# A graph-and-experts kernel: the second expert layer scales its rows by weights stored beside them and adds them into the output by accumulating scatters, without a last combining stage

## The reference, cut to what matters

```python
x = x + L0_gnn(layernorm(x))     # attention over heads of gathered rows
x = x + L0_ffn(layernorm(x))     # 6 experts, hidden 256, 256, the best 2 by softmax
x = x + L1_gnn(layernorm(x))     # GAT over 100000 edges, segment sums
x = x + L1_ffn(layernorm(x))     # 8 experts, hidden 1024, the best 2:
#   top_w, top_i = top_k(xf @ Wg + bg, 2);  top_w = softmax(top_w)
#   out = sum over e of w_dense[:, e] * (gelu(xf @ W1[e] + b1[e]) @ W2[e] + b2[e])
```

## Time and profile before

| | |
|---|---|
| runs (3), median | 2874.93 us (2872.90 to 2878.44) |
| profiled execution | 2876.24 us |
| its span, first to last instruction | 2874.6 us |
| busy in the span: TensorE / VectorE / ACT / POOL | 2056.5 / 1554.9 / 936.1 / 1426.2 us |
| mean granted TensorE clock | 0.822 |
| DMA | 293.06 MB, mean 102 GB/s |

### The profile page before, as it was taken

One profiled execution on the slowest core, in us unless ns is written; L12 is line 12 of the kernel. 1 busy time (PEld: TensorE's weight loads), 2 busy tenths in 40 slices (PEclk: granted clock), 3 DMA queues, 4 the chain that ended last, 5 costly groups with the idle time before them and its releaser, 6 DMA issues. The chain is left out here.

```text
span 2874.6 us, 54757 instructions
## 1 busy us (share of the span) xinstructions
PE 2056.5 (72%) x13130; PEld 1850.7 (64%) x13131; DVE 1554.9 (54%) x4111; ACT 936.1 (33%) x2579; POOL 1426.2 (50%) x1463
## 2 busy tenths in 40 slices
PE   2623328998475888877888788786519999999990
PEld 2423217898354666666666666665519999999990
DVE  5366525665473655555555555556624545555445
ACT  1333315676241111111111111112315555555540
POOL 1257753434104777777777777773761223232230
PEclk9855558999686888888888888886559999999995
DMA  6312243333353444444444444443251222121117
GB/s 157 102 45 78 76 116 92 105 102 98 105 169 93 112 112 114 112 114 114 112 114 113 110 115 112 112 114 87 103 141 46 72 73 73 55 91 51 62 37 268
DMA packets 234820, 293.06 MB, mean 102 GB/s; under 512 B 101917, under 2 KB 185524, under 8 KB 234540
## 3 DMA queue, kind: packets, MB, share of 16 engines
q0 software_dynamic: 72016, 202.56, 24.3%
q1 hardware_dynamic: 149222, 76.37, 10.5%
q10 hardware_dynamic: 13544, 13.73, 1.4%
HBM read 214.72 MB, written 78.22 MB: 102 GB/s over the span
## 5 line engine op out<-in xcount | busy, mean ns | idle before, releaser
L1553 POOL DMA_INDIRECT at_G<-h_as,at_idx x850 | 807.1, 950 | 269.2 <-issue 266.7
L1704 PE MATMUL at_pAgg<-at_G,at_OH 128*128 128x260 f32 x1700 | 542.6, 485 | 159.8 <-DVE at_ACC L1602 95.5
L1704 PEld LDWEIGHTS at_pAgg<-at_G,at_OH 128*128 128x128 f32 x1700 | 404.8, 246 | 261.5 <-DVE at_G L1584 179.0
L1169 POOL DMA_INDIRECT expert_out<-e_ob,e_to x212 | 221.6, 1045 | 560.6 <-DVE e_ob L1380 392.4
L1304 ACT ACTIVATE e_full<-e_pH,g_bias_hidden 128x256 f32<-128x256 f32 x640 | 316.0, 494 | 357.4 <-PE e_pH L1202 344.6
L1662 ACT ACTIVATE at_OT<-at_pTr 128x384 f32<-128x384 f32 (+1 forms) x300 | 125.7, 470 | 657.2 <-PE at_pTr L1689 656.9
L1364 DVE TENSOR_TENSOR e_hT_low<-e_full,e_hT_high 128x256 fp32r<-128x256 f32 x536 | 263.2, 503 | 130.6 <-ACT e_hT_high L1305 130.5
L1584 DVE TENSOR_TENSOR at_G<-at_G,at_pIds 128x1536 f32<-128x1536 f32 x150 | 249.7, 1665 | 153.5 <-ACT at_pIds L1669 153.5
L1200 PE MATMUL e_pH<-e_xT_high,e_WA_high 128*128 128x256 f32 x1072 | 309.1, 288 | 3.9 <-DVE e_WA_low L1359 3.0
L1201 PE MATMUL e_pH<-e_xT_low,e_WA_high 128*128 128x256 f32 x1072 | 306.8, 286 | 0.0
L1202 PE MATMUL e_pH<-e_xT_high,e_WA_low 128*128 128x256 f32 x1072 | 305.0, 285 | 0.0
(11 more groups left out here) (301 smaller groups left out, 3635.7 us busy)
## 6 DMA issues: line engine op xcount, KB each, us to landing
e_xs<-slot_rows SPq DMA_DIRECT2D x109, 257.0 KB
at_G<-h_as,at_idx POOLq DMA_INDIRECT x850, 2.8
b_rows<-expert_out SPq DMA_DIRECT2D x14, 896.0 KB
f_rows<-expert_out ACTq DMA_DIRECT2D x14, 896.0 KB, 6.9
g_raw_first<-in_L_ffn_W_dram POOLq DMA_DIRECT2D x8, 1024.0 KB, 5.3
g_raw_last<-in_L_ffn_W_dram POOLq DMA_DIRECT2D x8, 1024.0 KB
xt_ar<-a_og SPq DMA_DIRECT2D x7, 910.0 KB, 4.5
h_as<-b_og SPq DMA_DIRECT2D x7, 910.0 KB, 4.2
```

Of the source, the lines that this page charges most:

```text
L1169: gp.indirect_dma_start(K.YS, bass.IndirectOffsetOnAxis(ap=to[b][:, s:s + 1], axis=0), ob[b][:, s, :], None).then_inc(sent[b], 16)
L1553: gp.indirect_dma_start(G[j][:, c, :], None, K.T1, bass.IndirectOffsetOnAxis(ap=idx[j][:, c:c + 1], axis=0)).then_inc(gathered[j], 16)
L1704: last = nc.tensor.matmul(pAgg[:, 0:DIM + 4], OH[j][:, c, :], G[j][:, c, :], start=(j == 0 and c == 0), stop=(j == NJ - 1 and c == CHUNKS[ ...
```

## The change

The second layer's slots get rows of 261 numbers: 256 features, the output row, the two experts chosen and their two weights. So both copies of a row are the same, and both scatters of a trip go out together, without `move`; the weights are worked out trip by trip in `place`, with an Exp on ACT (`shares`). While b1 runs, SP stores `K.X` to the output. In e1 VectorE picks the share of the tile's expert, ACT scales the product by it (`scale`), VectorE adds the bias times the share, and POOL's scatter adds the rows into the output in DRAM; rows beyond the last node are left out by the bounds check. As two scatters may meet in one row, each waits until the one before has landed. `finish` is gone.

In both layers POOL's trip splits the last weights before it loads others, and waits for the landing of the previous tile's scatters in each tile ahead of its own, not at the end of a pair. VectorE notes the output rows earlier in its trip. In b0 the rows have two buffers, and its loops on SP and VectorE are written out.

```diff
-WIDE = DIM + 1
+TO, WHICH, SHARE = DIM, DIM + 1, DIM + 3
+WIDE0, WIDE1 = DIM + 1, DIM + 5
...
+K.XS = {tag: dram(f"slot_rows_{tag}", [DUMP + 2 * P, wide]) for tag, wide in (("e0", WIDE0), ("e1", WIDE1))}
+K.out = out
+K.YS = dram("expert_out", [2 * NODEROWS + 2 * MT, DIM])
...
-finish(K, out)
...
+rows = sb("rows", [P, 2, 2, BODY, DIM])
...
 def load_results(sp, i):
-    freed(sp, rows_used, i * BODY)
+    b = i % 2
+    if i >= 2:
+        freed(sp, rows_used, i - 1)
     for k in range(2):
         a = i * (BODY * P) + k * NODEROWS
-        at = slice(a, a + BODY * P) if isinstance(i, int) else bass.ds(sp.snap(a), BODY * P)
-        sp.dma_start(rows[:, k, :, :], K.YS[at, :].rearrange("(t p) d -> p t d", p=P)).then_inc(rows_in, 16)
+        sp.dma_start(rows[:, b, k, :, :], K.YS[a:a + BODY * P, :].rearrange("(t p) d -> p t d", p=P)).then_inc(rows_in[b], 16)
...
+if gate:
+    with sp.Fori(0, TRIPS - 1) as i:
+        r0 = sp.snap(i * (BODY * P))
+        freed(sp, y_kept, i * BODY + BODY)
+        sp.sem_inc(passed, 1)
+        sp.dma_start(K.out[bass.ds(r0, BODY * P), :].rearrange("(t p) c -> p t c", p=P),
+                     K.X[:, bass.ds(i * BODY, BODY), :]).then_inc(stored, 16)
+        sp.wait_ge(stored, sp.snap(i * 16 + 16))
+        sp.sem_inc(passed, 1)
+    a, t = (TRIPS - 1) * BODY * P, (TRIPS - 1) * BODY
+    freed(sp, y_kept, TRIPS * BODY)
+    sp.dma_start(K.out[a:a + (BODY - 1) * P, :].rearrange("(t p) c -> p t c", p=P), K.X[:, t:t + BODY - 1, :]).then_inc(stored, 16)
+    sp.dma_start(K.out[a + (BODY - 1) * P:NODES, :], K.X[0:TAIL, TILES - 1, :]).then_inc(stored, 16)
+    sp.wait_ge(stored, TRIPS * 16 + 16)
...
+if pre == "combine":
+    load_results(sp, 0)
+    load_results(sp, 1)
+    for i in range(TRIPS):
+        if i + 2 < TRIPS:
+            load_results(sp, i + 2)
+        store(i)
+        if i + 1 < TRIPS:
+            free(i)
...
-if k == 1:
+if router and k == 1:
     gp.wait_ge(moved, i + 1)
 for t in range(i * BODY, (i + 1) * BODY):
-    gp.indirect_dma_start(K.XS, bass.IndirectOffsetOnAxis(ap=K.POS[:, t, k:k + 1], axis=0),
+    gp.indirect_dma_start(XS, bass.IndirectOffsetOnAxis(ap=K.POS[:, t, k:k + 1], axis=0),
...
-for i in range(TRIPS + late + 1):
+for i in range(TRIPS + late + (1 if router else 0)):
     if pre == "attn0" and i < TRIPS:
         gather(i)
     if routed and 0 <= i - late < TRIPS:
         scatter(i - late, 0)
-    if routed and 0 <= i - late - 1 < TRIPS:
-        scatter(i - late - 1, 1)
+    n = i - late - (1 if router else 0)
+    if routed and 0 <= n < TRIPS:
+        scatter(n, 1)
...
+V = nc.vector
+b = i % 2
+v.wait_ge(rows_in[b], i // 2 * 32 + 32)
 for j in range(BODY):
-    Xt = K.X[:, tiles(t0 + j, 1), :].rearrange("p o d -> p (o d)")
-    Wt = K.WT[:, tiles(t0 + j, 1), :].rearrange("p o d -> p (o d)")
-    ch.mark(nc.vector.scalar_tensor_tensor(Xt, rows[:, 0, j, :], Wt[:, 0:1], Xt, ALU.mult, ALU.add))
+    ch.mark(V.scalar_tensor_tensor(K.X[:, t0 + j, :], rows[:, b, 0, j, :], K.WT[:, t0 + j, 0:1], K.X[:, t0 + j, :], ALU.mult, ALU.add))
 ch.settle()
 for j in range(BODY):
-    Xt = K.X[:, tiles(t0 + j, 1), :].rearrange("p o d -> p (o d)")
-    Wt = K.WT[:, tiles(t0 + j, 1), :].rearrange("p o d -> p (o d)")
-    nc.vector.scalar_tensor_tensor(Xt, rows[:, 1, j, :], Wt[:, 1:2], Xt,
-                                   ALU.mult, ALU.add).then_inc(rows_used, 1)
-freed(v, rows_used, i * BODY + BODY)
-v.sem_inc(passed, 1)
+    last = V.scalar_tensor_tensor(K.X[:, t0 + j, :], rows[:, b, 1, j, :], K.WT[:, t0 + j, 1:2], K.X[:, t0 + j, :], ALU.mult, ALU.add)
+last.then_inc(rows_used, 1)
+freed(v, rows_used, i + 1)
...
+if gate:
+    ch.mark(V.tensor_scalar(Y[:, tiles(t0, BODY), WHICH + k:WHICH + k + 1], r[:, :, :], -1.0, float(E), ALU.mult, ALU.add))
...
+if gate:
+    V.tensor_tensor(gap[:, :, :], top[:, :, 1:2], top[:, :, 0:1], ALU.subtract).then_inc(gap_in, 1)
...
+if gate:
+    v.wait_ge(gap_out, i + 1)
+    ch.link(V.tensor_scalar(share[:, :, :], gap[:, :, :], 1.0, None, ALU.add))
+    ch.link(V.reciprocal(share[:, :, :], share[:, :, :]))
+    ch.mark(V.tensor_copy(Y[:, tiles(t0, BODY), SHARE:SHARE + 1], share[:, :, :]))
+    ch.mark(V.tensor_tensor(Y[:, tiles(t0, BODY), SHARE + 1:SHARE + 2], gap[:, :, :], share[:, :, :], ALU.mult))
+    ch.settle()
 assert ch.n == placing, ch.n
-if not isinstance(i, int) or i > 0:
+if router and (not isinstance(i, int) or i > 0):
...
+def shares(n):
+    act.wait_ge(gap_in, n)
+    nc.scalar.activation(gap[:, :, :], gap[:, :, :], ACT.Exp).then_inc(gap_out, 1)
...
+if gate and j == BODY - 3:
+    with act.If(i > 0):
+        shares(i)
...
+def landed(n):
+    for s in range(SUB):
+        gp.wait_ge(sent[s], n * 16)
+    gp.sem_inc(passed, 1)
+def scatter(t, b):
+    for s in range(SUB):
+        freed(gp, o_ready, t * SUB + (s + 1))
+        if not deep and s > 0:
+            gp.wait_ge(sent[s - 1], t * 16 + 16)
+        gp.sem_inc(passed, 1)
+        at = bass.IndirectOffsetOnAxis(ap=to[b][:, s:s + 1], axis=0)
+        if deep:
+            gp.indirect_dma_start(K.YS, at, ob[b][:, s, :], None).then_inc(sent[s], 16)
+        else:
+            gp.indirect_dma_start(K.out, at, ob[b][:, s, :], None, bounds_check=NODES - 1, oob_is_err=False,
+                                  compute_op=ALU.add).then_inc(sent[s], 16)
...
+def trip(i, b):
+    t = i * 2 + b
+    freed(gp, tile_done, t + 1)
+    gp.sem_inc(passed, 1)
+    with begins(gp, t + 1):
+        e = expert(gp, t + 1)
+        split_last(e)
+        next_last(e)
+        if deep:
+            next_middle(e)
+        else:
+            next_first(e)
+    if deep:
+        with begins(gp, t + 2):
+            next_first(expert(gp, t + 2))
+    if b == 0:
+        with gp.If(i > 0):
+            landed(t)
+            gp.sem_inc(ob_free, 1)
+    else:
+        landed(t)
+        gp.sem_inc(ob_free, 1)
+    scatter(t, b)
...
-with gp.Fori(0, gp.snap(last_pair(gp) + 1)) as i:
-    for b in range(2):
-        t = i * 2 + b
-        freed(gp, tile_done, t + 1)
-        gp.sem_inc(passed, 1)
-        if deep:
-            with begins(gp, t + 2):
-                next_first(expert(gp, t + 2))
-        with begins(gp, t + 1):
-            e = expert(gp, t + 1)
-            if deep:
-                next_middle(e)
-            else:
-                next_first(e)
-            split_last(e)
-            next_last(e)
-        for s in range(SUB):
-            freed(gp, o_ready, t * SUB + (s + 1))
-            gp.sem_inc(passed, 1)
-            gp.indirect_dma_start(K.YS, bass.IndirectOffsetOnAxis(ap=to[b][:, s:s + 1], axis=0),
-                                  ob[b][:, s, :], None).then_inc(sent[b], 16)
-        if b == 1:
-            for c in range(2):
-                gp.wait_ge(sent[c], i * (16 * SUB) + 16 * SUB)
-                gp.sem_inc(ob_free[c], 1)
+last = last_pair(gp)
+with gp.Fori(0, gp.snap(last + 1)) as i:
+    trip(i, 0)
+    trip(i, 1)
+landed(last * 2 + 2)
...
-freed(pe, o_ready, t * SUB)
+freed(pe, o_ready if deep else scaled_ready, t * SUB)
...
+def scale(t):
+    at = slice(t, t + 1) if isinstance(t, int) else bass.ds(t, 1)
+    freed(act, o_ready, t * SUB)
+    freed(act, share_ready, t + 1)
+    freed(act, tile_done, t + 1)
+    for s in range(SUB):
+        nc.scalar.activation(scaled[:, s, :], pO[s][:, 0:DIM], ACT.Copy,
+                             scale=share[:, at, s:s + 1].rearrange("p o s -> p (o s)")).then_inc(scaled_ready, 1)
...
+if end and not deep:
+    scale(r)
...
-def keep_to(t, b):
+def shares(t, b):
+    at = slice(t, t + 1) if isinstance(t, int) else bass.ds(t, 1)
     freed(v, pX_ready, t + 1)
-    at = slice(t, t + 1) if isinstance(t, int) else bass.ds(t, 1)
-    V.tensor_copy(to_all[:, at, :].rearrange("p o s -> p (o s)"), xs[b][:, :, DIM]).then_inc(to_ready, 1)
-def o_out(i, b):
-    t = i * 2 + b
+    if deep:
+        V.tensor_copy(to_all[:, at, :].rearrange("p o s -> p (o s)"), xs[b][:, :, TO]).then_inc(to_ready, 1)
+        return
     e = expert(v, t)
-    freed(v, ob_free[b], i)
+    freed(v, share_ready, t)
+    V.scalar_tensor_tensor(picked[:, :, :], xs[b][:, :, WHICH:WHICH + 2], K.iota[:, bass.ds(e, 1)], xs[b][:, :, SHARE:SHARE + 2],
+                           ALU.is_equal, ALU.mult).then_inc(picked_ready, 1)
+    v.wait_ge(picked_ready, t + 1)
+    V.tensor_reduce(share[:, at, :].rearrange("p o s -> p (o s)").rearrange("p (s o) -> p s o", o=1),
+                    picked[:, :, :], AX.X, ALU.add).then_inc(share_ready, 1)
+    V.tensor_copy(to_all[:, at, :].rearrange("p o s -> p (o s)"), xs[b][:, :, TO]).then_inc(to_ready, 1)
+def o_out(t, b):
+    e = expert(v, t)
+    v.wait_ge(ob_free, t + 1)
     freed(v, to_ready, t + 1)
     V.tensor_copy(to[b][:, :], to_all[:, bass.ds(t, 1), :].rearrange("p o s -> p (o s)"))
-    freed(v, tile_done, t + 1)
+    if deep:
+        freed(v, tile_done, t + 1)
     for s in range(SUB):
```

(78 more changed lines are left out.)

147 lines of the change are left out of this document (52 added, 95 removed).

## The result

The changed kernel takes 2796.61 us (median of 4 runs, 2794.77 to 2799.11) against 2874.45 (4 runs) for the kernel before beside it: a ratio of 0.9728, 95% interval 0.9711 to 0.9745. The forecast was 2800. The profiled execution took 2799.11 us with a span of 2797.5: 77.1 less than before, where the sum of the prediction had 75. The sum is close, but three of its terms have the wrong sign, and the two large misses (14.2 us better, 10.7 us worse) mostly cancel.

The account below looks back on a forecast made before the run. TensorE bounds the second expert stage, while 77.0 us follow the last product uncovered. Terms -66 - 8 - 1 + 2 - 2 = -75 on the span of 2874.6 give 2799.6, so 2800 for a median; range 2780 to 2830.

Parts of the forecast that it names:

- Tail, -66: Behind TensorE's last product: 11 us would stand where 77.0 stood, as loads, VectorE operations and stores go.
- The accumulating scatter: Second expert stage: landing taken as 3.3 us, between bounds of 2.6 and 5.4, hidden up to 4.6.
- the signs that I had named as making the prediction wrong: A landing above 4.6 us, VectorE's gate trip above 17.7, or the accumulating instruction holding POOL much longer than 0.97.
- Rival 1: Second expert stage: landing between a tile's two scatters becomes the bound; 2889 us at 5.4 landing; one in twelve.
- Combining, -8: Where results are combined: two row buffers cut VectorE's 14.9 us of row waits, some of 1 to 2 returning.
- Gate stage, -1: Gate stage: `move` goes, VectorE's trip grows to about 16.5 us, POOL stays the bound; ends -5 and +8.
- First expert stage, +2: First expert stage: POOL's pair 0.35 us longer, +7 in all, against -5 from the earlier split of weights.
- one more wait with its restart: First expert stage, POOL: each tile's landing wait costs 1.6 + 0.9 us, less 0.7 of control beside it.
- Second expert stage, -2: Second expert stage: earlier split at seven changes of expert gives -5 us, a late output buffer after changes +3.
- Covered, by 0.2 us: Second expert stage: ACT frees its first hidden-unit buffer at 2.6 us, before TensorE's fifth unit is due at 2.9.
- rival 2: Expert stages: new work on ACT (+14) or POOL (+11) stalls TensorE, giving 2812 to 2828 us; one in five.
- Rivals 2 and 3: Besides rival 2, the third: split wait, first expert stage and combining give back more, 2778 to 2786; one in six.

Follow-up runs that it names:

- e_together: Changed kernel, but the two accumulating scatters of one tile go out without a wait between them: 2787.22 us against the changed kernel's 2796.67.
- e_no_add: Changed kernel, but the second expert layer's scatters write rows instead of adding them: 3341.34 us against 3429.18 for the kernel before (0.9746).
- e_old_order: Changed kernel, but POOL again loads the next weights before splitting the last ones, in both layers: ratios to the kernel before 0.9814 and, run again, 0.9791.
- e_pair_landing: Changed kernel, but in the first expert layer POOL waits for landings at a pair's end: ratios to the kernel before 0.9785 and, run again, 0.9817.
- e_x_first: Changed kernel, but in the second expert layer ACT copies the next tile's rows before scaling the product: 3340.45 us against 3407.73 for the kernel before (0.9802).

## Why the prediction was right, point by point

- **Tail, -66, measured -61.6.** The mechanism held; mis-sized are two terms. The wait of the first scatter for the previous tile's landing was left out (+1.9), and what follows the last landing takes 4.7 in place of 2. (The terms that I gave for the first scatter also add up to 2.4, not 2.6.)
- **The accumulating scatter.** The median landing is 3.8, between the bounds and under the limit of 4.6. Two of the signs that I had named as making the prediction wrong did show: six landings of 7.2 to 8.3, and an instruction that holds POOL for 1.55 in place of 0.97. The second was harmless since POOL had room. Rival 1 did not happen in the steady tiles. Behind two changes of expert its mechanism did, for single tiles with landings of 8 us; I had allowed 3 us for that, and it and the landing's share of other tiles cost 5.8 by `e_together` (the stage of `e_no_add` gives as much). The Trainium skill (Collectives: The Full Stack, The bandwidth ceiling) says of a reduce-scatter between cores that its add needs two source reads, which halves the throughput. Here the landing grows by a factor of 1.6 (2.4 to 3.8), which agrees in direction; no run separates reads from writes.
- **Combining, -8, measured -11.6.** Right in kind; the second buffer won 8.3 and the loops 3.3, where I let waits of 1 to 2 us come back. Two did, of 0.95 and 0.77. The split between buffer and loops is rough, as said above.
- **Gate stage, -1, measured +1.0.** VectorE's trip is 16.2 on average (16.5 forecast), and POOL stayed the bound. The first scatter came 5.8 later than before, counted from the last gather, in place of 3.9. By the rule of the Trainium skill that I cited (ScalarE: Activation LUTs, Table sets) a change costs 2.7 us; here three loads of 1.28 stand in each trip, and the next activation starts 0.01 after a load ends. By the rule the trip would be 18, an estimate; it is 16.2, so the measurement decides against it.
- **First expert stage, +2, measured -12.2.** This is the step that failed. I took POOL's pair to be 0.35 longer: "one more wait with its restart" beside 3.0 of control in series. The control runs while the scatter lands, so a trip is 4.70 and not 5.25 (gaps of 2.46 each, not 2.9 and 3.3). The wait for the weights falls by 13.5, where I had 5 and gave it to the order of the split alone. Both edits lower it: with the landing by tile alone 14 of the 24.8 are left (`e_old_order`), with the order alone 15 to 17 (`e_pair_landing`). But only with the landing by tile does the stage get shorter. And I missed both the clock (-6.9) and the long tiles (some +1.1 on 17), which take back what the order wins.
- **Second expert stage, -2, measured +8.7.** "Covered, by 0.2 us" failed by a little in every second tile. ACT's first unit starts at 1.9 (1.8 forecast) but takes 0.84, where I had 0.73, so its buffer is free at 2.8 in place of 2.6, just when TensorE comes to its fifth unit; and units that follow at 0.72 leave TensorE no slack. `e_x_first` gives 4.8 back. This is rival 2, at half its price of 14 (0.25 on every second tile is 6.8). Why only every second tile: ACT's branch at the end of a pair lies ahead of it, which I argue from the order and did not try. By `e_together` the accumulating landings cost 5.8, and by `e_old_order` the earlier split wins 4: 632.7 + 4.8 + 5.8 - 4 = 639.3, against 638.7 measured. The rest of the 8.7 is ahead of the first product (from the first transposes 19.3 in place of 17.3, and 0.7 until these).
- **Rivals 2 and 3** both came true in part. Against their forecasts, four parts of the table came out 19 us better in all and three 17 us worse. That the sum hit is in good part luck: the terms behind the tail were forecast at -9 in all and measured at -15.5, but one by one they missed by up to 14 us.

## What to carry to other kernels

A wait for a landing that stands in an issuing engine's loop makes the trip as long as that landing, and anything that lands with it can lengthen it and then hold the phase; give the wait to the one who needs the buffer. A cover of 0.2 us beside an in-order engine is none: move what can run early ahead of the wait. And price a wait at a change of weights with the clock behind it: here 13.5 us less of such waits came with 6.9 us less for the same matmuls.

## What the runs showed of the hardware

- An indirect scatter of 128 rows of 1 KB that adds holds POOL for 1.55 us, the plain one for 0.97; a bounds check adds nothing to that (1.55 with it and without). Median landing: 3.8 against 2.4.
- A plain scatter's landing is 2.4 us in most tiles, and 3.5 to 4.1 in every one of the 107 tiles (of 459, nine profiles) where a 257 KB load is issued 0.26 to 0.62 us behind it. Behind two loads of 1 MB, with the add or without, it is 7 to 8.
- In the first expert stage of the two kernels the granted clock fell to 0.50 (1.2 GHz) during each of seven waits for the last weights of 4.0 to 6.4 us, for 3.4 to 10.2 us, and at none of the three such waits of 0.4 to 0.6.
- On two of the chips the attention takes some 1540 us for the same 850 gathers, elsewhere 1065. Between 1000 and 1500 us ACT waited there (`e_old_order_2`) 225.0 us in 16 places (up to 14.5) for something the profile calls remote, and the same line 130 us for TensorE; in the changed kernel's own profile that line waited 304.9 us, for TensorE alone. What the remote wait is stays open:

```profile
ACT at_OT L1784 <- remote: 225.0, 16, 14.5
```
